# First loads in another order, keys of the first batch projected first, all engine orders rewritten

## What is computed

```
x = x + xattn(layernorm(x), ctx, ctx, mask)       # x: 8 x 512 x 512, ctx: 8 x 120 x 512
x = x + ffn(layernorm(x))

xattn: Q = xn @ wq + bq; K = ctx @ wk + bk; V = ctx @ wv + bv    # 16 heads of 32
       scores = Q K^T / sqrt(32); scores = where(mask == 0, 1e-9, scores)
       out = (softmax(scores) V) @ wo + bo
ffn:   h = gelu(bitlinear(x, w1, b1)); y = bitlinear(h, w2, b2)
bitlinear: rows of rmsnorm(x) rounded to 8 bits by their own largest value,
           weights rounded to -1, 0, 1 by the mean of |w| over the whole matrix
```

## Time and profile before

| what | value |
|---|---|
| median of 3 runs | 652.19 us (651.63 to 652.81) |
| the profiled execution | 650.6 us |
| its span, first to last instruction | 648.8 us |
| PE busy | 628.9 us (97%) |
| DVE busy | 574.3 us (89%) |
| ACT busy | 530.2 us (82%) |
| POOL busy | 518.7 us (80%) |
| granted TensorE clock, mean | 1.00 |

### The profile page before, as it was taken

One profiled execution on the slowest core, in us unless ns is written; L12 is line 12 of the kernel. 1 busy time (PEld: TensorE's weight loads), 2 busy tenths in 40 slices (PEclk: granted clock), 3 DMA queues, 4 the chain that ended last, 5 costly groups with the idle time before them and its releaser, 6 DMA issues.

```text
span 648.8 us, 14114 instructions
## 1 busy us (share of the span) xinstructions
PE 628.9 (97%) x4904; PEld 423.7 (65%) x4904; DVE 574.3 (89%) x1062; ACT 530.2 (82%) x1450; POOL 518.7 (80%) x653
## 2 busy tenths in 40 slices
PE   8988999999999999999999999999999999999996
PEld 6746886666666676766666676666667666565542
DVE  5697889999999988999899988999889799999894
ACT  2579679987889888887898878888988889998674
POOL 3297977979977898688967899778959778999776
PEclk9999999999999999999999999999999999999999
DMA  8983310424315443354224343043333122543236
GB/s 291 402 300 111 126 41 9 107 45 106 84 28 115 103 91 75 38 135 90 71 67 114 74 121 74 10 132 87 90 74 74 24 75 41 128 86 88 62 61 182
DMA packets 109286, 65.38 MB, mean 101 GB/s; under 512 B 90856, under 2 KB 90856, under 8 KB 108576
## 3 DMA queue, kind: packets, MB, share of 16 engines
q1 hardware_dynamic: 108159, 64.49, 37.9%
q10 hardware_dynamic: 1056, 0.00, 0.1%
HBM read 35.12 MB, written 8.39 MB: 67 GB/s over the span
## 4 chain that ended last, share of the span: by engine, by line
PE 67%; POOL 13%; DVE 8%; DMA 4%; ACT 4%; issue 3%; SPq 0%; POOLq 0%; DVEq 0%; ACTq 0%
PE ps_a L573 23%; PE ps_y L710 11%; PE ps_z L687 11%; PE ps_t L646 6%; PE ps_s L636 4%; PE ps_a L658 3%; POOL hid L2270 2%; POOL prob L2259 2%; DMA q_hT<-q_h 2%; PE ps_y L580 2%; DVE hs L1633 2%; POOL q_h L2275 2%; PE ps_a L607 2%; ACT prob L1145 2%; DMA wk_s<-in_L_xattn_wk_dram 1%
## 5 line engine op out<-in xcount | busy, mean ns | idle before, releaser
L1145 ACT ACTIVATE prob<-ps_s,nmax 128x120 f32<-128x120 f32 x512 | 178.9, 377 | 24.7 <-DVE nmax L1579 19.2
L2259 POOL TENSOR_TENSOR prob<-prob,pinv 128x480 f32<-128x480 f32 x128 | 129.2, 1017 | 41.0 <-DVE pinv L1584 40.0
L687 PE MATMUL ps_z<-w1T,q_xT 128*128 128x512 fp8e4 x476 | 122.8, 380 | 0.5 <-DVE hid L1625 0.4
L1145 ACT ACTIVATION_READ_ACCUMULATOR prob<-ps_s,nmax 128x1 f32 x512 | 113.3, 221 | 0.0
L710 PE MATMUL ps_y<-w2T,q_hT 128*128 128x512 fp8e4 x448 | 105.5, 379 | 1.5 <-DMA q_hT<-q_h 1.5
L1625 DVE SCALAR_TENSOR_TENSOR hid<-ps_z,y_deq,b_row 128x512 f32<-128x512 f32 x119 | 88.0, 739 | 10.6 <-PE ps_z L687 9.2
L1576 DVE COPY_PREDICATED_SCALAR ps_s<-hidden_key,masked_c 128x480 f32 x128 | 90.5, 707 | 4.2 <-PE ps_s L636 3.9
L1121 ACT COPY probT<-ps_t 120x512 f32<-120x512 f32 x128 | 76.9, 601 | 15.4 <-PE ps_t L646 14.3
L1579 DVE TENSOR_REDUCE nmax<-ps_s 128x4 f32<-128x480 f32 x128 | 84.1, 657 | 4.4
L646 PE MATMUL ps_t<-ident,prob 128*120 128x128 f32 x512 | 77.9, 275 | 4.3 <-POOL prob L2259 3.7
L646 PEld LDWEIGHTS ps_t<-ident,prob 128*120 128x120 f32 x512 | 60.0, 137 | 25.3 <-issue 7.4
(11 more groups left out here) (207 smaller groups left out, 1373.7 us busy)
## 6 DMA issues: line engine op xcount, KB each, us to landing
x<-in_x_dram SPq DMA_DIRECT2D x32, 256.0 KB, 2.9
out_dram<-x SPq DMA_DIRECT2D x32, 256.0 KB, 2.8
xn<-in_x_dram SPq DMA_DIRECT2D x7, 1024.0 KB, 6.6
hid<-in_L_ffn_w_dram SPq DMA_DIRECT2D x4, 1024.0 KB, 9.6
ctx_k<-in_ctx_dram SPq DMA_DIRECT2D x8, 240.0 KB, 3.1
ctx_k<-in_mask_Bx1xSxS_ik_dram SPq DMA_DIRECT2D x7, 240.0 KB, 3.1
xn<-in_x_dram SPq DMA_DIRECT2D x4, 256.0 KB, 3.5
x<-in_L_xattn_wq_dram SPq DMA_DIRECT2D x1, 1024.0 KB, 7.3
```

Of the source, the lines that this page charges most:

```text
L687: last = nc.tensor.matmul(bank[:], q_xT[:, k % 3, i], w1T[:, i, c * CH:(c + 1) * CH], start=(i == 0), stop=(i == KD - 1))
L1145: last = nc.scalar.activation(prob[:, n % 3, g * S2:(g + 1) * S2], ps_s[n % HG][:, g * S2:(g + 1) * S2], ACT.Exp, bias=nmax[:, n % 4, g:g ...
L2259: gp.tensor_tensor(pr, pr, pinv[:, n % 4].unsqueeze(2).to_broadcast([P, HG, S2]), ALU.mult).then_inc(s["prob_ready"], 1)
```

## The change

The steps are the same ones in all lists, except that PE issues 50 `keep_busy` transposes where it issued 60. What changes is their order.

- SP: the context comes first, then x tiles 1 and 0, wk, x tiles 2 and 3, piece 2 of w1, and only then wq; pieces 0 and 1, the first mask and piece 3 follow. Later issues are moved against each other by a few places.
- PE: 20 and 30 `keep_busy` stand around the transposed context; the keys of batch 0 are projected ahead of the x tiles' transposes; `turn_keys(0)` stands behind the first third of the first queries.
- DVE: `split_wq` goes behind the low parts of x; `hide(0)` goes ahead of `weight_scales(0)`; `add_bk(0)` goes behind it.
- In the loop, SP's `load_x(a + 2)` goes ahead of `turn_h(4 * a - 4)`; PE's `ffn_down(4 * a - 4, 0)` keeps its place behind `turn_xn(a + 1, 3)`, with `project_out`, `project_ctx(a + 1, "v")`, two `ffn_up`, three `turn_probs` and `attend` between them.
- All lists are rewritten in the loop and the tail as well, by moves of a few places.

The core of the diff (the rest are moves within the same lists, most of them by one to three places):

```
 SP, first loads
-            for t in range(T):
-                sp.dma_start(xn[:, t], xt_v[0, t]).then_inc(s[f"first{t}_in"], 16)
             load_first_ctx()
+            load_first_x(1)
+            load_first_x(0)
+            load_wk()
+            load_first_x(2)
+            load_first_x(3)
+            load_piece(2)
             load_wq()
-            load_wk()
+            load_piece(0)
             load_piece(1)
-            load_piece(0)
+            load_first_mask()
             load_piece(3)
-            load_piece(2)
             load_x(1)
             load_wo()
-            load_first_mask()
+            load_next_ctx()
             load_wv()
+            load_bv()
             load_piece(4)
-            load_next_ctx()
-            load_bv()
 SP, loop
             for a in range(2, 6):
...
+                load_x(a + 2)
                 turn_h(4 * a - 4)
-                store(4 * a - 5)
-                load_x(a + 2)
 PE
             pe.wait_ge(s["consts_pool"], 2)
-            keep_busy(40)
+            keep_busy(20)
             turn_ctx(0)
-            keep_busy(20)
+            keep_busy(30)
+            project_ctx(0, "k")
             turn_xn(0, 0)
             turn_xn(0, 1)
             turn_xn(0, 2)
-            project_ctx(0, "k")
             turn_xn(0, 3)
+            first_q(0)
             turn_keys(0)
-            first_q(0)
             first_q(1)
             first_q(2)
...
             turn_ctx(1)
+            turn_piece(1, (0, 1))
             turn_probs(0)
-            turn_piece(1, (0, 1))
             turn_piece(1, (2, 3))
...
             ffn_up(28, 1)
             turn_probs(125)
-            ffn_down(26, 0)
             ffn_up(28, 2)
             ffn_up(28, 3)
             turn_probs(126)
             project_out(30)
+            ffn_down(26, 0)
             turn_probs(127)
             ffn_down(26, 1)
 ACT
+            evac_turn(("x", 0, 3))
             evac_keys(0)
-            evac_turn(("x", 0, 3))
-            evac_q(0, 0)
             sum_abs(0)
             sum_abs(2)
+            evac_q(0, 0)
 DVE
             xT_low(0, 0)
-            split_wq()
             xT_low(0, 1)
             xT_low(0, 2)
             xT_low(0, 3)
+            split_wq()
+            scale_bq()
             sum_abs(1)
-            add_bk(0)
-            scale_bq()
             sum_abs(3)
+            hide(0, mask0_in)
             weight_scales(0)

             ln1_stats(1, 0)
             ln1_stats(1, 1)
+            add_bk(0)
             ln1_stats(1, 2)
             ln1_stats(1, 3)
-            hide(0, mask0_in)
             softmax_max(0)
             evac_piece(0, 1)
             split_wo()
+            softmax_max(1)
             invert_sums(0)
             evac_piece(0, 3)
-            softmax_max(1)
             softmax_max(2)
...
             evac_up(28, 0)
+            ln2_stats(29)
             invert_sums(126)
-            evac_down(25)
-            ln2_stats(29)
             evac_up(28, 1)
+            oT_low(30)
+            invert_sums(127)
             ln2_scales(29)
-            invert_sums(127)
-            oT_low(30)
             evac_up(28, 2)
             evac_up(28, 3)
+            evac_down(25)
             h_scale(27)
 POOL
             round_piece(2)
+            ln1_apply((0, 1))
             normalize(1)
-            ln1_apply((0, 1))
             ln1_apply((2, 3))
             round_piece(3)
```

More of the change, by code:

```diff
@@ L820, in _ @@
             project_out(1)
+            turn_probs(11)
             turn_piece(7, (2, 3))
-            turn_probs(11)
             project_q(1, 3)
             ffn_up(0, 0)
-            turn_ctx(2)
             turn_probs(12)
@@ L830, in _ @@
             turn_probs(13)
-            turn_xn(2, 0)
+            turn_ctx(2)
             ffn_up(0, 2)
             turn_probs(14)
+            turn_xn(2, 0)
             ffn_up(0, 3)
             project_out(2)
+            ffn_up(1, 0)
             turn_probs(15)
             turn_xn(2, 1)
-            ffn_up(1, 0)
             project_ctx(2, "k")
+            turn_xn(2, 2)
             turn_probs(16)
@@ L970, in _ @@
             ffn_down(19, 0)
-            ffn_down(19, 1)
+            ffn_up(21, 2)
             turn_probs(96)
             attend(23)
+            ffn_down(19, 1)
+            ffn_up(21, 3)
+            turn_probs(97)
             turn_xn(7, 2)
-            ffn_up(21, 2)
             scores(25)
-            turn_probs(97)
-            ffn_up(21, 3)
             project_out(23)
@@ L983, in _ @@
             project_ctx(7, "v")
+            ffn_up(22, 1)
             turn_probs(99)
-            ffn_up(22, 1)
-            turn_probs(100)
-            attend(24)
             ffn_down(20, 0)
             ffn_up(22, 2)
+            attend(24)
+            turn_probs(100)
+            ffn_down(20, 1)
+            turn_probs(101)
             project_q(7, 0)
-            turn_probs(101)
             ffn_up(22, 3)
-            ffn_down(20, 1)
             scores(26)
@@ L998, in _ @@
             project_q(7, 1)
-            turn_keys(7)
             turn_probs(103)
             ffn_up(23, 1)
+            turn_keys(7)
+            turn_probs(104)
             attend(25)
-            turn_probs(104)
+            ffn_down(21, 0)
             ffn_up(23, 2)
-            ffn_down(21, 0)
             scores(27)
@@ L1022, in _ @@
             turn_probs(110)
+            ffn_up(24, 2)
             project_out(26)
@@ L1976, in _ @@
                 residual(4 * a)
-                invert_sums(16 * a + 8)
+                softmax_max(16 * a + 11)
+                ln2_stats(4 * a)
+                evac_up(4 * a - 1, 0)
+                ln2_scales(4 * a)
                 invert_sums(16 * a + 9)
-                softmax_max(16 * a + 11)
-                add_bk(a + 1)
-                evac_up(4 * a - 1, 0)
+                h_scale(4 * a - 2)
                 ln1_stats(a + 2, 3)
+                hide(a + 1, mask_in)
                 invert_sums(16 * a + 10)
-                hide(a + 1, mask_in)
```

876 lines of the change are left out of this document (438 added, 438 removed).

## The result

The changed kernel takes **658.17 us** (median of 4 runs, 657.51 to 658.81) where the kernel before took 651.91 beside it (651.04 to 652.81): ratio **1.0103**, 95% interval 1.0091 to 1.0115. Forecast were 652.0, with a range of 649.7 to 654.5.

What follows compares the result with a forecast made beforehand. PE, busy for 97% of the span, was taken as the bound. Prologue +1.0, middle 0 and tail -1.2 sum to -0.2, giving 652.0 us for the median; range 649.7 to 654.5.

Steps and rivals of the forecast that it cites:

- The middle: From 60 to 540 us: same matmuls, so a round stays at 74.41 and the term is 0.
- the bound of 2.2: Middle: PE's 2.2 us of waits may all go, or as many come.
- The prologue: First 60 us: later wq, piece 3 and scale of w1 make PE +1.0 late, bounds -1.9 and +3.1.
- The tail: Behind the loop: DVE's 1.66 us hole at 604.07 closes, gelu(27) is late next, -1.2; bounds -1.66 and +1.66.
- Rival 1: Prologue, middle and tail: PE's waits are filled, -2.2, 650.0 us; chance 0.34.
- Rival 2: 27 to 42 us: DVE becomes the late engine through hide(0) and softmax_max(1), +1.9, 654.1 us; chance 0.15.
- Rival 3: Loop: turn_h(4a-4) over 7 us behind load_x on SP, PE waits about 1 us in four rounds, 655.8; chance 0.10.
- the cover that the forecast worked out: Loop: turn_h(4a-4)'s 7.3 us behind load_x hidden by 32 matmuls of 7.4 us and four smaller steps.
- Rival 4: Prologue: PE's pauses around x's transposes lower the clock, first queries slower, +1.0, 653.0 us; chance 0.05.
- Rival 5: Prologue loads: queue not landing in issue order shifts first queries up to 2.86 us either way; chance 0.02.

Runs made afterwards that it cites:

- e6: Changed kernel with SP's load_residual(4a+3) moved back ahead of turn_h(4a-1) in the loop: ratio 1.0061 to the kernel before, 2.7 us back.
- e15: Kernel before with the changed loop alone, but load_residual(4a+3) ahead of turn_h(4a-1) again: ratio 1.0017, where the changed loop alone made 1.0042.
- e5: Changed kernel with DVE's split_wv moved five steps down behind residual(5), away from split_wk: ratio 1.0088 to the kernel before, 1.0 us back.
- e8: Changed kernel with unread identity transposes in PE's pauses ahead of turn_piece(3) (12) and turn_probs(27) (20): ratio 1.0092 to the kernel before.
- e12: Kernel before with the new prologue, plus identity transposes in PE's pauses ahead of first_q(0) (14) and turn_piece(3) (12): ratio 1.0013.
- e10: Changed kernel with the old middle, load_residual(4a+3) moved back in the loop, and three PE pauses filled with transposes: ratio 1.0045, 2.9 us slower.

## Why the prediction was wrong

**The middle was the step that failed.** "The lists hold the same matmuls, so a round stays at 74.41 ... I take 0" counted PE's work and left the waits at their old size. The stretch that it calls the middle is what the experiments split into "middle" and "loop". The one alone costs 2.9 and the other 2.7; each is beyond the bound of 2.2 that was set for both. A round is no longer the one before: from `project_out(10)` to `project_out(14)` it takes 75.58 in place of 75.03, and the next 75.76 in place of 74.41. Two places make most of it. In the loop it is `load_residual(4a+3)` behind `turn_h(4a-1)` on SP, shown by moving this one step back (e6, e15). In the middle it is `split_wv` next to `split_wk` on DVE with `round_h(2)` of POOL under them, shown by the rows of two kernels and by e5 for the wait (2.90 to 0.78) and by e8 for the clock (1.5 us), but not by a time, as e5 loses 1.4 elsewhere. "The stores and residual loads beside it move tiles that are wanted many steps later; I cost them at nothing" looked at who needs the moved tile, and not at what stands behind it in the queue: `turn_x(4a+1)`, which had landed 0.45 us ahead of its use before (328.88 against 329.33).

**The prologue** was right in its chain and short in sizes. The first x tiles and wk landed about 1 us later than worked out (last x tile 11.39 for 10.4, wq 17.27 for 16.1); behind them a transfer of 1024 KB takes 2.5 to 3.2, where 2.86 was assumed. So `first_q(0)` came at 19.34 and not 18.1, and the first queries ended 1.5 late and not 0.2. The scale came at 28.77 (28.2 said), POOL's rounding at 29.48 (28.9), piece 3's transposes at 54.20 (53.7); `hide(0)` took 0.40 (0.38 said). With the clock PE is 2.2 late at 66 us, where 1.0 was said. Measured alone it is +0.9, so the term's size holds at the end of the program, but by luck: PE is 2.6 late at 66 us in that run, and old waits behind it absorb a part, which the prediction had ruled out ("paid in full, since no slack follows").

**The tail** was right in mechanism: the hole of 1.66 closed. PE is 1.3 less late at the end than at `project_out(23)`, as the -1.2 said; but what is late next is not `gelu(27)`: it is `turn_x(31)`, and the clock behind its pause takes the gain back in some executions. By the ratio it is -0.5, or -0.8 with the pause filled.

**Rivals.** Rival 1 did not occur as a whole: PE's waits grew; only between `project_out(0)` and `project_out(5)` did the new order gain, 1.1 us. Rival 2 occurred by half and cost nothing at its end: `hide(0)` took 0.40 and not 1.10, but `turn_ctx(1)` was held 0.82 us by DVE at 41.39 and PE was 2.9 late there, but only 1.2 at `project_ctx(1, "k")`. Rival 3 came nearest to the time (655.8 of 658.2; its own sum of 652.0 and four waits of 1 makes 656.0), by a mechanism that the changed kernel's trace shows to be absent: its condition, over 7 us for the transpose, held, and the cover that the forecast worked out held as well. The chance of 0.10 had the right queue and the wrong step of it. Rival 4, given 0.05, happened, but mostly at other places than it named, and its +1.0 is not what came: in the profiled execution the first queries ran at full clock, and the clock fell behind the waits for piece 3 (0.9 us) and at `turn_probs(27)` (1.5 us), where no pause was foreseen. Of eight executions with the new prologue and its wait for wq left bare, seven had a granted clock under 1.00 in the first 60 us, two of them on the first queries; of eight with the old one, two. In the time, filling the pauses of the prologue changed nothing (e12). Rival 5 did not: all transfers landed in order of issue.

The range's upper end of 654.5 would have held the prologue and the tail as they came. What carried the time out of it is the 5.6 us between 67 and 500 us, for which the only case set up was rival 3. No run undid all of it: with every place found mended, 1.7 us stay unexplained (e10).

## What to carry to other kernels

When lists are rewritten by small moves, the moved step's own cost is the wrong thing to look up: for every move, name what now stands next to it on another engine's port, and what stands behind it in its queue and how much slack that has. A place with 0.45 us of slack on the critical engine is a place to look at even if the diff changes only a residual load there. And price a pause of PE at its length plus what the clock cost here (0.9 to 1.6 us), with a chance, and fill what can't be closed; whether that shows in the time depends on what waits behind it.

## What the runs showed of the hardware

POOL and DVE: a POOL pass over 128x2048 that normally takes 1.98 us stood at 6.03 beside two successive DVE operations of 2.3 us with two SBUF inputs, in all seven executions that had them back to back (6.02 to 6.04), and at 3.89 beside one. POOL did not get in between the two. It goes the other way round as well: in the kernel before, `split_wk` took 3.40 in place of 2.3 when it began 0.64 behind the start of a POOL pass (152.43 to 154.33). The Trainium skill (SBUF — State Buffer, Who interferes with whom) describes the pair of ports that these engines share as an exclusive lock for the length of an instruction; the rows agree, and add that the waiting engine need not be next.

TensorE's clock: behind waits of 1.6 to 2.9 us PE ran at 1.2 in place of 2.4 GHz for a stretch, at a price of 1.5 to 1.6 us where matmuls stood close (`project_q(2, 3)` 4.35 for 2.77, eight `ffn_up` matmuls 3.47 for 1.90) and of 0.9 behind piece 3. It did not happen every time: behind the wait of 2.9 us at `turn_probs(27)` it did in all six executions that had it bare, but the same wait of 2.35 us ahead of `ffn_up(31, 0)` was followed by a granted clock of 0.96 from 600 to 645 us in five executions and of 1.00 in four. Transposes whose result nobody reads, in the wait, kept the clock at 1.00 there in both executions that had them. The Trainium skill (TensorE: Matmul & The Clock Gate, HAM oscillation) has a PE that idles between bursts fall back to half clock; here that was so for single pauses of this length, in a part of the executions.
